# Four buffers for the copied C and its spread apart from B's, the last block's weights and x loaded inside its first pipeline, and attentions' value products in two halves

## What is computed

```python
x = x + attn0(ln(x)); x = x + moe0(ln(x))       # 16 heads of 8, then 16 small experts
x = x + attn1(ln(x)); x = x + block1(ln(x))     # causal with rotary positions, then a whole block
x = x + mamba(ln(x)); x = x + moe2(ln(x))       # selective scan, then 8 experts
x = x + attn3(ln(x)); x = x + lora3(ln(x))      # two corner scores masked
```

```python
xs    = silu(conv4(x @ W_in[:, :256]) + conv_b);  z = x @ W_in[:, 256:]
d, Bp, Cp = split(xs @ W_x, [1, 16, 16]);  delta = softplus(d * w_dt + b_dt)
h[t]  = exp(delta[t] * A) * h[t-1] + delta[t] * xs[t] * Bp[t]     # per channel and state
y[t]  = sum over states of h[t] * Cp[t]
out   = ((y + xs * D) * silu(z)) @ W_out
```

## Time and profile before

| | us |
| --- | --- |
| median of 3 runs | 3947.56 (3946.97 to 3956.48) |
| profiled execution | 3950.09 |
| its span | 3948.3 |
| TensorE busy | 3142.3 (80%) |
| VectorE busy | 2337.4 (59%) |
| ScalarE busy | 1703.3 (43%) |
| GpSimd busy | 866.3 (22%) |

### The profile page before, as it was taken

How to read it: one execution, slowest core, us unless ns; L and a number is a source line. 1 busy time by engine, 2 the same in 40 slices (tenths; PEclk the granted TensorE clock), 3 DMA queues, 4 the chain that set the end, 5 groups by cost and what they waited for, 6 DMA issues and landing times. The chain is left out here.

```text
span 3948.3 us, 49284 instructions
## 1 busy us (share of the span) xinstructions
PE 3142.3 (80%) x18104; PEld 1596.1 (40%) x18112; DVE 2337.4 (59%) x4715; ACT 1703.3 (43%) x3002; POOL 866.3 (22%) x920
## 2 busy tenths in 40 slices
PE   4988977748888397979784777767799996998977
PEld 1222224424444275656561222222377774222224
DVE  5777858856776234343423778888633234777754
ACT  1776741105556132323222454444433332576752
POOL 3222123422220000000001555555500001111001
PEclk9999987759999597989896888888899997899998
DMA  3101000001221100000002000000000000111100
GB/s 100 28 22 33 17 1 1 1 16 37 39 39 23 58 1 11 5 6 6 6 11 80 0 0 0 0 0 0 0 1 1 1 1 17 35 33 22 28 1 22
DMA packets 74519, 69.79 MB, mean 18 GB/s; under 512 B 10536, under 2 KB 72368, under 8 KB 72752
## 3 DMA queue, kind: packets, MB, share of 16 engines
q1 hardware_dynamic: 71216, 66.35, 7.3%
q10 hardware_dynamic: 3072, 0.40, 0.1%
HBM read 22.02 MB, written 6.29 MB: 7 GB/s over the span
## 5 line engine op out<-in xcount | busy, mean ns | idle before, releaser
L394 DVE TENSOR_REDUCE a_mx<-banks 128x1 f32<-128x512 f32 (+3 forms) x1536 | 870.7, 616 | 326.5 <-PE banks L654 200.9
L527 ACT ACTIVATE a_prob<-banks 128x512 f32<-128x512 f32 (+3 forms) x1536 | 776.0, 546 | 436.1 <-PE banks L677 206.6
L677 PE MATMUL banks<-a_Qs,a_Ks 64*128 64x512 bf16 (+3 forms) x1536 | 506.1, 363 | 108.3 <-ACT a_prob L527 101.0
L654 PE MATMUL banks<-a_Ks,a_Qs 63*128 63x512 bf16 (+3 forms) x1536 | 479.0, 370 | 28.0 <-DVE a_mx L394 15.6
L1590 PE MATMUL banks<-m_hc,kc 128*128 128x512 f32 x512 | 322.7, 735 | 124.0 <-POOL m_hc L1468 99.7
L1468 POOL TENSOR_TENSOR m_hc<-m_h,m_cs 128x512 f32<-128x512 f32 x256 | 326.6, 1294 | 305.9 <-DVE m_h L1399 305.9
L1104 ACT ACTIVATE b_room<-banks,w_b 128x512 f32<-128x512 f32 x256 | 176.0, 688 | 480.7 <-PE banks L1071 479.7
L703 PE MATMUL banks<-a_prob,a_vaug 128*32 128x512 f32 (+3 forms) x3072 | 376.3, 562 | 2.9 <-ACT a_prob L527 2.9
L1399 DVE TENSOR_TENSOR_SCAN m_h<-banks,m_u 128x512 f32<-128x512 f32 x256 | 300.7, 1207 | 27.5 <-ACT banks L1513 27.5
L654 PEld LDWEIGHTS banks<-a_Ks,a_Qs 63*128 63x128 bf16 x1536 | 130.6, 95 | 399.3 <-DVE a_mx L394 239.7
L677 PEld LDWEIGHTS banks<-a_Qs,a_Ks 64*128 64x128 bf16 x1536 | 132.2, 93 | 357.6 <-ACT a_prob L527 281.6
(11 more groups left out here) (322 smaller groups left out, 4400.9 us busy)
## 6 DMA issues: line engine op xcount, KB each, us to landing
a_Ks<-a_parts SPq DMA_DIRECT2D x288, 64.0 KB
a_Qs<-a_parts SPq DMA_DIRECT2D x288, 64.0 KB
w_c<-in_pc SPq DMA_DIRECT2D x5, 1024.0 KB
w_b<-in_pb SPq DMA_DIRECT2D x4, 1024.0 KB
a_Qs<-a_negm ACTq DMA_DIRECT2D x192, 2.0 KB
w_a<-in_pa SPq DMA_DIRECT2D x2, 1024.0 KB
xres<-in_x SPq DMA_DIRECT2D x8, 256.0 KB, 4.2
x<-xres SPq DMA_DIRECT2D x8, 256.0 KB
```

Of the source, the lines that this page charges most:

```text
L394: dve.tensor_reduce(mx[:, g % 2, col:col + 1], M[:, k % 3, 0:keys[j]], AX.X, ALU.max).then_inc(S("max_read"), 1)
L527: act.activation(prob[:, n % 8, first_query[kt]:T], Sc[:, n % 2, first_query[kt]:T], ACT.Exp, scale=scale).then_inc(S("exped"), 1)
L654: i = pe.matmul(M[:, k % 3, 0:keys[j]], Qs[lo:lo + LAST, b % 4, pair, j * P:(j + 1) * P], Ks[lo:lo + LAST, b % 4, pair, 0:keys[j]], start= ...
L677: i = pe.matmul(Sc[:, n % 2, q0:T], Ks[lo:lo + HALF, b % 4, pair, kt * P:(kt + 1) * P], Qs[lo:lo + HALF, b % 4, pair, q0:T], start=True, s ...
```

## The change

1. **C in four buffers, and its order.** `cs` has four buffers, so that the copy of step k waits for GpSimd's products of step k-4. The C copy is due at at(k) - 1.8 in place of -2.8. The C spread is due at at(k) - 2.0, while the B spread stays at -3.4.
2. **Loads.** PACK_C is cut after `wout` (2288 columns); the rest (9882 columns) is PACK_D in a tensor `w_d` of its own. `load_all` goes. `mamba_all` gets an SP lane that issues the eight x loads, one semaphore for each, and then w_d; the statistics of batch b wait for its x. moe2, a3 and lora3 read w_d.
3. **Value products in halves.** Where a block is wider than 256 columns it is made in two halves, the second two steps after the first. The semaphore `av_done` is raised by the last half.

```diff
-                        gp.tensor_tensor(hc[:, n % 6, :], h[:, n % 4, :], cs[:, k % 2, :],
+                        gp.tensor_tensor(hc[:, n % 6, :], h[:, n % 4, :], cs[:, k % 4, :],
...
-                        yield at(k) - 2.8
+                        yield at(k) - 1.8
                         act.wait_ge(S("c_spread"), k + 1)
-                        if k >= 2:
-                            act.wait_ge(S("weighed"), NCH * (k - 1))
-                        act.activation(cs[:, k % 2, :], Cs, ACT.Copy).then_inc(S("c_taken"), 1)
+                        if k >= 4:
+                            act.wait_ge(S("weighed"), NCH * (k - 3))
+                        act.activation(cs[:, k % 4, :], Cs, ACT.Copy).then_inc(S("c_taken"), 1)
...
+                    for k in range(DS * B):
+                        yield at(k) - 3.4
                         pe.matmul(Bs, kb("sel32", 96)[:, n:n + 1].broadcast_to([96, P]), G[:, b % 2, :], start=True,
                                   stop=True).then_inc(S("b_spread"), 1)
+                        yield at(k) - 2.0
                         if k:
                             pe.wait_ge(S("c_taken"), k)
                         pe.matmul(Cs, kb("sel32", 96)[:, DS + n:DS + n + 1].broadcast_to([96, P]), G[:, b % 2, :],
                                   start=True, stop=True).then_inc(S("c_spread"), 1)
...
+                def sync_loads(sp):
+                    tensor, src = later
+                    n = tensor.shape[1]
+                    for b in range(B):
+                        yield float(b)
+                        sp.dma_start(xres[:, b, :, :], x_view[:, b, :, :]).then_inc(S("x_loaded_%d" % b), 16)
+                    for a in range(0, n, 2048):
+                        yield 20.0 + a / 1000
+                        sp.dma_start(tensor[:, a:min(n, a + 2048)], src[:, a:min(n, a + 2048)]).then_inc(S("later_loaded"), 16)
+                    sp.wait_ge(S("later_loaded"), 16 * -(-n // 2048))
...
+                def value_halves(kt):
+                    q0 = first_query[kt]
+                    return [(q0, T)] if T - q0 <= 256 else [(q0, (q0 + T) // 2), ((q0 + T) // 2, T)]
...
-                        q0 = first_query[kt]
+                        q0, q1 = spans[half]
                         for hl in range(GH):
-                            i = pe.matmul(V[32 * hl:32 * hl + 32, g % 2, q0:T], vaug[:, b % 3, kt, g % NG * GH + hl, :],
-                                          prob[:, (4 * a + hl) % 8, q0:T], start=kt == 0, stop=kt == NT - 1,
+                            i = pe.matmul(V[32 * hl:32 * hl + 32, g % 2, q0:q1], vaug[:, b % 3, kt, g % NG * GH + hl, :],
+                                          prob[:, (4 * a + hl) % 8, q0:q1], start=kt == 0 and half == 0, stop=kt == NT - 1,
                                           skip_group_check=True)
-                        i.then_inc(S("av_done"), 1)
+                        if half == len(spans) - 1:
+                            i.then_inc(S("av_done"), 1)
...
-                        if 0 <= a < 16 * B and r == 0:
+                        if 0 <= a < 16 * B and r in (0, 2) and r // 2 < len(value_halves(a % NT)):
                             yield at(s) + 0.1
-                            values(a)
+                            values(a, r // 2)
```

More of the change, by code:

```diff
@@ L58 @@
 PACK_C = [("win", 512), ("convw", 8), ("convb", 2), ("convr", 1024), ("wxd", 256), ("wxp", 192),
-          ("wdt", 2), ("bdt", 2), ("alog", 32), ("dcol", 2), ("wout", 256), ("gw", 8), ("eb", 8),
+          ("wdt", 2), ("bdt", 2), ("alog", 32), ("dcol", 2), ("wout", 256)]
+PACK_D = [("gw", 8), ("eb", 8),
           ("wup", 4096), ("wdn", 4096), ("wq3", 128), ("wk3", 128), ("wv3", 128), ("wo3", 128),
@@ L152, with build @@
 ENGINES = ("vector", "gpsimd", "scalar", "sync", "tensor")
-def build(nc, x, pa, pb, pc, pk, pkb, b2, out):
+def build(nc, x, pa, pb, pc, pd, pk, pkb, b2, out):
     top = ExitStack()
@@ L688, in mask_score, with values @@
                                   start=False, stop=True).then_inc(S("scored"), 1)
-                    def values(a):
+                    def values(a, half):
                         g, kt = divmod(a, NT)
                         b = g // NG
[L693 to L700, removed]
-                        q0 = first_query[kt]
+                        spans = value_halves(kt)
+                        if half == 0:
+                            pe.wait_ge(S("exped"), 4 * (a + 1))
+                            if kt == 0:
+                                if g % NG == 0:
+                                    pe.wait_ge(S("v_ready"), b + 1)
+                                if g >= 2:
+                                    pe.wait_ge(S("o_normed"), g - 1)
+                                if g % NG == 1 and b:
+                                    pe.wait_ge(S("done"), b)
+                        q0, q1 = spans[half]
                         for hl in range(GH):
-                            i = pe.matmul(V[32 * hl:32 * hl + 32, g % 2, q0:T], vaug[:, b % 3, kt, g % NG * GH + hl, :],
-                                          prob[:, (4 * a + hl) % 8, q0:T], start=kt == 0, stop=kt == NT - 1,
+                            i = pe.matmul(V[32 * hl:32 * hl + 32, g % 2, q0:q1], vaug[:, b % 3, kt, g % NG * GH + hl, :],
+                                          prob[:, (4 * a + hl) % 8, q0:q1], start=kt == 0 and half == 0, stop=kt == NT - 1,
                                           skip_group_check=True)
-                        i.then_inc(S("av_done"), 1)
+                        if half == len(spans) - 1:
+                            i.then_inc(S("av_done"), 1)
                     k = 0
@@ L1340, in build, with mamba_all @@
             staggered(early_b, late_b, T // 128)
-        def mamba_all(xres, wc, wconv, acoef):
+        def mamba_all(xres, wc, wconv, acoef, x_view, later):
             STEP, LEAD = 4.0, 58.0
@@ L1404, in vector_batch @@
                     yield t
+                    dve.wait_ge(S("x_loaded_%d" % b), 16)
                     if b:
@@ L1576, in spread @@
                                   start=True, stop=True).then_inc(S("c_spread"), 1)
-                    for k in range(DS * B):
-                        yield at(k) - 3.4
-                        spread(k)
                 def tensor_sums(pe):
@@ L1811, in build @@
             load_weights([(w_c, pc)])
+            w_d = sb(ctx, "w_d", [P, width(PACK_D)])
+            wd = Pieces(w_d, PACK_D)
             def prepare(block):
@@ L1828, in build @@
             out_b = out.rearrange("(b t p) c -> p b t c", b=B, p=P)
[L1829 to L1837, removed]
+            mamba_all(xres, wc, wc("convr"), acoef, x2_b, (w_d, pd))
             with ExitStack() as inner:
@@ L1844, in plan_m @@
                         st.buf["x"] = xres[:, b]
[L1845 removed]
+                        yield moe2(st, wd, "moe2_%d_" % b)
                 round_of([(s, plan_m) for s in range(2)], OFFSET_C)
[L1849 to L1850 removed]
+            c3 = wd("cols3")
+            attention_all("a3_", xres, (wd("wq3"), wd("wk3"), wd("wv3"), wd("wo3"), c3[:, 0:1], c3[:, 1:2], wd("bv3")),
                           float(HD) ** -0.5, 0.62, corners=True)
@@ L1867, in plan_l @@
                         st.buf["x"] = xres[:, b]
-                        program, length, done = lora3(st, wc, "lora_%d_" % b)
+                        program, length, done = lora3(st, wd, "lora_%d_" % b)
                         yield program, length, done
@@ L1979 @@
         "dcol": chunked(a["L2_attn_D"]), "wout": chunked(a["L2_attn_W_out"]),
+    }
+    pd = {
         "gw": a["L2_ffn_gate_w"].T, "eb": row(a["L2_ffn_expert_bias"]),
@@ L1988 @@
     arrays = {"x": np.ascontiguousarray(a["L0_attn_x"].reshape(B * T, C)), "pa": packed(pa, PACK_A),
-              "pb": packed(pb, PACK_B), "pc": packed(pc, PACK_C), "pk": tables, "pkb": tables_b,
+              "pb": packed(pb, PACK_B), "pc": packed(pc, PACK_C), "pd": packed(pd, PACK_D), "pk": tables, "pkb": tables_b,
               "b2": np.ascontiguousarray(a["L1_ffn_b2"])}
@@ L1994 @@
     out = nc.dram_tensor("out", (B * T, C), F32, kind="ExternalOutput").ap()
-    build(nc, *(handles[k] for k in ("x", "pa", "pb", "pc", "pk", "pkb", "b2")), out)
+    build(nc, *(handles[k] for k in ("x", "pa", "pb", "pc", "pd", "pk", "pkb", "b2")), out)
     r = run_bass_kernel_spmd(nc, [{f"in_{k}": v for k, v in arrays.items()}], core_ids=[0])
```

5 lines of the change are left out of this document (2 added, 3 removed).

## The result

| | before | after |
| --- | --- | --- |
| median of 4 runs, us | 3947.77 (3946.97 to 3956.48) | 3893.82 (3891.68 to 3896.35) |
| profiled execution, us | 3950.09 | 3896.35 |
| its span, us | 3948.3 | 3894.6 |

The ratio after/before is 0.9859 with a 95% interval of 0.9844 to 0.9874: 54 us faster, inside the range, 18 us above the forecast of 3876.

The account below looks back on a forecast made before the run. In the attentions no engine was full and VectorE and ScalarE waited for TensorE; the scan waited on spreads and decays. From 3950.1: -19.6 + 24.5 - 36 - 36 - 5 = -72, 3878; median 2.5 lower, 3876; range 3825 to 3930.

Parts of the forecast that it names:

- Loads: Before the scan stage: -12.0 us for w_d's transfer and -7.6 for the earlier first statistics, sum -19.6.
- Buffers alone: In the scan: four buffers of C by themselves change the time by 0.
- Moves in the scan: Later C spread on TensorE and C copy on ScalarE: 3.5 us x 7 periods, +24.5 us.
- the first step: In a scan period: C spread falls behind the convolution product L1610; everything up to two mag/pos pairs comes 1.4 us later.
- the second: In a scan period: C copy runs only after the first decay; next C spread 3.3 us later, m_u 3.1 later.
- rival B: In the scan: the clock falls in the longer idle before the C spread, +48 for +24.5, 3899 us; chance 0.12.
- Halves in a0 and a3: In the two attentions without a mask: value products in halves gain 36 us each.
- The step that held all of it: In unmasked attentions: TensorE returns 0.43 us sooner per half block; 0.38 taken for three blocks in four.
- Halves in a1: In the masked attention, half the blocks split: -5 us, between +9 and -28.
- C: Rival: halves gain their whole bound, 55 + 55, and the masked attention 20: -130 for -77, 3823 us; chance 0.13.
- D: Rival: in the attentions the gap only moves to ScalarE's two score banks, -20 in all, 3933 us; chance 0.10.
- E: Rival: TensorE's own time paces the attentions; split pairs cost 0.14 us each, +45, VectorE's waits grow, 3998 us; chance 0.05.

Follow-up runs that it names:

- e1: The changed kernel with only its loads kept: value blocks whole, two buffers of C, both due times as before; 3934.85 us, ratio 0.9955.
- e4: The changed kernel with the due times of C spread and C copy put back, four buffers kept; 3863.24 us, ratio 0.9774.
- e5: The changed kernel with only the C spread's due time put back, the C copy staying late; 3869.41 us, ratio 0.9785.
- e11: The changed kernel with the scan's due times back and both halves of a value block one right behind the other; 3936.42 us in one run.
- e10: The changed kernel with only the second convolution product moved, due at t+12.1 in place of t+11.5; 3863.34 us in one run.
- e12: The kernel of e8 with value blocks in three parts (176, 168, 168 columns) in the attentions without a mask; 3889.38 us, ratio 0.9841.
- e6: The changed kernel with only the C copy's due time put back, the C spread staying late; 3888.44 us in one run.
- e13: The kernel of e8 with a batch's preparation begun one step earlier and spread over more scan steps; 3843.83 us, ratio 0.9728.
- e8: The changed kernel with the scan's old due times and halves only in the attentions without a mask; 3859.9 us, ratio 0.9768.

## Why the prediction came out as it did

- **Loads: right.** -12.0 for the transfer was 12.0; -7.6 for x was 7.0. w_d's traffic beside the scan was priced at the lower of two bounds, 0, and e1 shows it.
- **Buffers alone: right, 0** (e4 against e1: 0.5 us).
- **Moves in the scan: size right, second half of the mechanism wrong, so that the closeness of the size is luck.** +24.5 was said, +22.2 came; a period of 92 us, and table loads in the same place are 91.8 and 92.5 us apart, in turn. Right was the first step: the C spread falls behind the convolution product, the copy, the table load and the SiLU chain with it, some 1.4 us; m_u's wait there went from 2.87 to 4.33, +1.46. Wrong was the second, "and the copy only then": it would have given a C spread 3.3 and an m_u 3.1 later. The timeline has the copy at 2510.16, ahead of the table load, the C spread's wait unchanged at 3.15 where I had said near 5, and e5 shows that the copy's due time alone costs nothing. I had read its place from a number, without seeing that the decays come from the same lane. What filled the room, in a period of 92.5: +1.40 after L1634 at half clock, where a wait of 2 to 3 us had been named; m_u waits 3.96 us in place of 3.11 behind the output product, +0.85, and 0.22 more in an earlier step. With the 1.46 these are 3.93; 0.29 less in a fourth wait leaves 3.64, about the 3.7 by which this period grew. In a period of 91.8 the wait behind the output product is 3.19, and the period grew by 3.1; no run shows why only every second one has the 0.85. The half clock is what rival B foresaw, from the earlier trace rows, at +3.3 a period on top of all the rest. It came, and cost 1.40, but not for B's reason, a longer idle time before the C spread: that stayed at 3.15. By its time of 3899 B lies nearer to the 3893.8 measured than the forecast does; by the scan stage, +22.2 against B's +48, it is out.
- **Halves in a0 and a3: right**, 38.0 and 36.6 for 36 each. The waits for L659 came out at 48.5 us for the 50 named. The step that held all of it, 0.43 us in which TensorE comes back sooner, is what e11 takes away, and the whole gain goes with it.
- **Halves in a1: wrong sign.** -5 was said, +9.8 came, 0.8 beyond the bound of +9, and this is most of the 18 us by which the forecast was too low. The term that was mis-sized is the gain: I took -5 between +9 and -28 without a row that showed a wait which a returning TensorE would end. The -28 came from giving all 64 pairs the 0.43 of the stage without a mask. The loss of 0.14 for each of 64 pairs accounts for 9 at most; e10 and e4, with the same halves, lose only 1 to 3 against the kernel before, little more than the scatter of 1.7 us among whole blocks. What lies on top goes with the granted clock, 0.93 to 0.89. That the lower clock makes the stage longer, and not some third thing both, was not separated, so the cause of the 9.8 us stays open.
- The rest of the 18: B and moe0 7.6 us longer, of the size of their scatter, and small parts (a0 and a3 gained 2.6 more and the scan lost 2.3 less than forecast; loads and lora3 took 1.6 more).
- Of the rivals, C (the whole bound of 55 in each attention) and D (-20 in all) are out by a0 and a3; E is out for halves; for thirds its size fits and its sign doesn't (e12).

The Trainium skill ("TensorEngine Tiling (Array Packing)", Key Properties) says that changing the tiling mode drains the array, which I had set against the halves. The rows agree that going over to the value products and back has a price, and put it at 0.14 us a trip: a pair of halves takes 1.00 us in one go and 2 x 0.57 in two (e11, after). Whether all of that is the drain, they don't say. With halves the price didn't show in the time: TensorE was busy 388.57 of 430 us before and 371.80 of 390 after, so it had idle time for the 18 us. With thirds it did (e12).

On the table load, the Trainium skill ("ScalarE: Activation LUTs", What ACT_TABLE_LOAD costs) speaks of a drain of some 1.38 us beside the load. In the kernel after the copy ahead of it ends at 2510.77, the load starts at 2510.79 and the decay behind it at 2512.08, 1.29 later: no drain shows here either.

## What to carry to other kernels

Where an engine serves short requests of others and one long block, look at how long it is away: cutting the block so that it comes back in between gained 38 us of 519 with no work removed, and one cut more lost 15 to 18 of it. Ask per stage whether the waiting engine would be served by that return; in the masked stage no run showed a gain. When a due time is moved, list what it now passes on its own queue, and what cannot pass because it comes from the same lane; two instructions that changed places cost 20 us here, and moving the other one's due time by 0.6 brought them back.

## What the runs showed of the chip beyond expectation

- The same instructions in a1 took from 444.5 to 453.8 us, at a mean granted clock from 0.92 to 0.89, in kernels that differ only in stages that come later (e10, e4, e6, after, e5). Whole value blocks took 442.6 to 444.3 at 0.93. There is one profile of each, so this can be scatter between executions: the four runs of e4 take 3855.0 to 3875.6, the longest at the lowest granted clock (0.888 against 0.892 to 0.893).
- After the same 3.15 us of idle time TensorE's next product ran at the upper level (1.88 us, six of seven periods before) or at the lower (3.39 to 3.46 us, all seven after). The idle time just ahead doesn't fix the level.
- Sixteen value matmuls of 256 columns in one go hold TensorE as long as eight of 512: 1.00 us.
- In e13 TensorE's work is the same as in e8 and the stage is shorter, but its clock is lower, 0.80 for 0.85: a shorter stage can have the lower clock. What that costs in time was not separated.
